# Two rotating mask tiles in place of three in a fused decoder layer, the freed space left empty

## The chip, the core and the metric

The kernel runs on one core of a Trainium2 chip. The metric is the device time of one execution in microseconds (us). The kernel before took 1540.39 us as the median of three runs (1539.06 to 1541.62). That is the figure that every change is measured against.

## What is computed

One decoder layer for 16 sequences of 100 tokens, width 128, against a context of 1444 rows per sequence. The reference, cut to its three residual steps:

```python
x = x + attn(layernorm(x), WQ, WK, WV)                  # banded self attention
x = x + xattn(layernorm(x), ctx, ctx, mask, W_Q, ...)   # 16 heads of 64, 1444 keys
x = x + ffn(layernorm(x), Wg, W1, ...)                  # 16 experts, top 2, and a shared one

def xattn(input_Q, input_K, input_V, attn_mask, ...):
    scores = einsum('bhqd,bhkd->bhqk', Q, K) / sqrt(64)
    scores = where(attn_mask[:, None, :, :], -10000.0, scores)
    return einsum('bhqk,bhkd->bhqd', softmax(scores), V) ... @ W_out.T + b_out
```

The mask is an input with one byte for each sequence, query and key: 16 x 100 x 1444.

## The kernel before

**Stages.** First the weights of the two attentions are folded together (`first_*`), then comes the cross attention of the 16 sequences, called batches here, one period of some 82 us each, and last the expert network. Self attention is worked off beside the cross attention, two sequences at a time, in what the code calls units: unit 0 in the first stage, unit 1 in the period of batch 0, units 2 to 7 each from an even batch into the odd one after it.

**Tiles.** The 1600 rows of a batch's score matrix (100 queries by 16 heads) are cut into 12 tiles of 128 rows, 8 queries by 16 heads, and one of 64 rows. So there are 13 tiles in a batch and 208 in all. For each tile, in this order:

- SP loads the tile's mask bytes, 128 x 1444 (180.5 KB), each query's row repeated for the 16 heads (`load_mask`, L900).
- POOL makes `bias = mask * -1e30 + c` from it (`make_bias`, L991). `bias` has two tiles of its own.
- PE makes the scores in two halves (L1257), DVE adds the bias and takes the row minimum of each half (L1142), ACT takes the exponential (L1073), POOL normalises (L1013, L1015), PE transposes the result (L1273), ACT and DVE split it into a high and a low part (L1082, L1157), and PE multiplies it by the context (L1297).

**The mask tiles rotate.** `MSLOTS` (L50) is their number, three. Tile n, counted through all batches, lies in slot n mod `MSLOTS`. Its load waits until the bias that read the slot's previous mask is made, which is the bias of tile n - `MSLOTS`; POOL's bias waits for the load by a semaphore of the slot.

**Order on the engines.** Each engine's order is fixed when the program is written: `ORDER` and the functions `act_order`, `dve_order` and `pool_order` lay it out by position in a period. DVE's list puts the statistics of unit 1 (`stat1`, L412) between the two halves of batch 0's first tile, and they wait for the unit's rows of x, `unit_x`. SP runs its list of loads and stores in order, and a load that waits holds back all that stands behind it. That list is `emit` under `@block.sync` (L910 to L946). The mask load of tile t stands first in step t, and the other transfers of the step behind it:

```python
def load_mask(b, t):                                              # L894
    n = b * NT + t
    wait(sp, bias_ready, n, 1, 1 - MSLOTS)                        # at least n + 1 - MSLOTS biases made
    sp.dma_start(masks[n % MSLOTS][0:rows_of(t), :], ...)
for t in range(NT):                                               # L916
    if here(b, 0):
        load_mask(b, t)
    if t == 2 and b == 0:
        load_context(1)                        # nat: 704 KB and three small pieces, L275, L278
        store_x1(sp, w, 0, x1_dram)            # unit 0's rows leave unit_x, L483
        load_x(sp, w, 1, x)                    # unit 1's rows enter it, once the store has landed, L490
        load_x1(0, 0)
    if t == 2 and 1 <= b <= CHUNKS // 2:
        clear(2 * b - 2)                       # waits for a POOL step behind the bias of tile 1
```

Behind later mask loads of a batch stand, in odd batches, the store of a unit's normalised rows (step 5, `store_n2`, L497) and the turn of its row constants through DRAM (step 6, `turn_c`, L504, L506, which PE reads at L367); in all, the load of the next batch's query rows (step 7, `load_rows`, L512, which PE reads at L1318) and a second `clear` (step 8). The next batch's context is loaded at the start of a period.

Of the kernel before, what the change touches and what calls it, by code (L numbers as in the profile page):

```python
# [46 lines left out]
NSTEP = len(STEPS)  # L47
PSLOTS = 6
TSLOTS = 3
MSLOTS = 3  # L50
QROUNDS = H // 2
PREP = 3 + QROUNDS
UNIT_AT = (11.5, 14.5, 16.5, 23.5, 36.2, 11.5, 14.5, 36.2)
# [6 lines left out]
def rows_of(t):  # L60
    return 128 if t < FT else HALF
# [723 lines left out]
def attention(nc, x, ctx_in, mask, wq_s, wk_s, wv_s, W_Q, b_Q, W_K, b_K, W_V, b_V, W_out, b_out,  # L785
# [4 lines left out]
    with ExitStack() as ctx:  # L790
        def sb(name, shape, dt=F32):
            return ctx.enter_context(nc.sbuf_tensor(name, shape, dt))

        def sem(name):
            return ctx.enter_context(nc.semaphore(name))

        def pair(name, shape, dt=F32):
            return [sb(f"{name}{i}", shape, dt) for i in range(2)]
# [6 lines left out]
        x1 = pair("x1", [S, D])  # L805
        masks = [sb(f"mask{i}", [128, SK], U8) for i in range(MSLOTS)]
        bias = pair("bias", [128, SKP])
# [14 lines left out]
        x1_in = [sem("x1_in0"), sem("x1_in1")]  # L822
        mask_in = [sem(f"mask_in{i}") for i in range(MSLOTS)]
        ctx_split = sem("ctx_split")
# [45 lines left out]
        def wait(engine, sem, b, per, plus):  # L870

            if b * per + plus > 0:
                engine.wait_ge(sem, b * per + plus)
# [7 lines left out]
        with nc.Block() as block:  # L881
            @block.sync
            def _(sp):
# [10 lines left out]
                def load_mask(b, t):  # L894
# [3 lines left out]

                    wait(sp, bias_ready, n, 1, 1 - MSLOTS)
                    sp.dma_start(masks[n % MSLOTS][0:rows_of(t), :],  # L900
                                 mask[b, q0:q0 + nq, :].unsqueeze(1).to_broadcast([nq, H, SK]))\
                        .then_inc(mask_in[n % MSLOTS], 16)

# [50 lines left out]
            def _(pool):  # L954
# [24 lines left out]
                def emit(b, odd):  # L979
                    def make_bias(db, t):  # L980
# [4 lines left out]
                        if t == 0:  # L985

                            pool.wait_ge(w.c_set, bb // 2 + 1)
                        pool.wait_ge(mask_in[m % MSLOTS], 16 * (m // MSLOTS + 1))

# [1044 lines left out]
```

## Time and profile before

| | us |
|---|---|
| median of three runs | 1540.39 |
| the profiled execution | 1540.29 |
| its span, from the first to the last instruction | 1538.1 |
| PE (matmuls) busy in it | 1439.2 |
| DVE busy | 1132.7 |
| POOL busy | 990.6 |
| ACT busy | 882.0 |

The profiled execution is one of the kernel's ordinary ones: it lies 0.1 us from the median. Some 2.2 us lie outside of its span. The page says for each engine how long it was busy, and in 40 slices of the span when. What an engine waited for is in the view of waits, and the order of single instructions in the timelines.

### The profile page before, as it was taken

What the parts mean: (1) busy time and instruction counts of PE and PEld (TensorE: products, weight loads), DVE (VectorE), ACT (ScalarE), POOL (GpSimd) and SP (SyncE); (2) the same over time, 40 slices, a digit from 0 to 9 for tenths busy, and PEclk for the clock granted to TensorE, in tenths of its full rate; (3) what the DMA queues carried; (4) which work ended last, traced back from release to release, by engine and by line L of the source; (5) the groups of instructions that cost most, each with busy time, mean ns of one, the idle gap of its engine ahead of it and who ended that gap; (6) DMA issues with size and microseconds to landing.
All of it is one profiled execution on the core that took longest, in us unless ns stands there. A gap on an engine that the chain in (4) does not pass through costs nothing. (4 is left out here: it accounts for less than half of the span.)

```text
span 1538.1 us, 30012 instructions
## 1 busy us (share of the span) xinstructions
PE 1439.2 (94%) x10546; PEld 1381.0 (90%) x10546; DVE 1132.7 (74%) x2768; ACT 882.0 (57%) x1663; POOL 990.6 (64%) x1127
## 2 busy tenths in 40 slices
PE   7799999999999999999999999999999999966696
PEld 6699999999999999999999999999999999955585
DVE  4687777777787877787877777777878686758565
ACT  2465666656565656565656656566656565616453
POOL 4675767666675757575757676766767675426564
PEclk8899999999999999999999999999999999967898
DMA  4211111111111111121111111111111101024322
GB/s 107 60 49 48 54 41 54 39 42 56 36 58 47 55 37 45 45 62 36 59 45 57 36 55 36 48 45 30 54 43 49 38 30 35 4 77 144 84 64 90
DMA packets 99981, 80.45 MB, mean 52 GB/s; under 512 B 16905, under 2 KB 98650, under 8 KB 99834
## 3 DMA queue, kind: packets, MB, share of 16 engines
q1 hardware_dynamic: 95098, 73.11, 16.1%
q0 software_dynamic: 2112, 4.29, 0.8%
q8 instruction: 85, 1.39, 0.4%
q10 hardware_dynamic: 2624, 1.14, 0.3%
q14 instruction: 62, 0.51, 0.1%
HBM read 67.37 MB, written 11.15 MB: 51 GB/s over the span
## 5 line engine op out<-in xcount | busy, mean ns | idle before, releaser
L1082 ACT CAST pT_hi<-banks 128x512 fp32r<-128x512 f32 (+1 forms) x672 | 362.4, 542 | 297.4 <-PE banks L1273 292.1
L1157 DVE TENSOR_TENSOR pT_lo<-banks,pT_hi 128x512 fp32r<-128x512 f32 (+1 forms) x576 | 360.2, 626 | 232.5 <-ACT pT_hi L1082 228.0
L1013 POOL TENSOR_SCALAR probs<-probs,row_inv 128x1408 f32<-128x1408 f32 x192 | 279.3, 1455 | 225.5 <-DVE row_inv L1149 225.3
L1273 PE MATMUL banks<-ident,probs 128*128 128x128 f32 (+1 forms) x2304 | 366.3, 274 | 18.9 <-DVE pT_lo L1157 9.6
L991 POOL TENSOR_SCALAR bias<-mask,c_all 128x1444 f32<-128x1444 uint8 (+1 forms) x208 | 307.0, 1476 | 118.3 <-DVE nmax L1142 107.5
L1073 ACT ACTIVATE probs<-probs,nmax 128x1448 f32<-128x1448 f32 x192 | 289.8, 1509 | 79.1 <-DVE nmax L1142 78.7
L1297 PE MATMUL banks<-pT_hi,ctx_hi 128*128 128x256 f32 (+1 forms) x1056 | 325.5, 308 | 0.3 <-DVE ctxT_lo L1183 0.3
L1273 PEld LDWEIGHTS banks<-ident,probs 128*128 128x128 f32 (+1 forms) x2304 | 266.9, 139 | 40.9 <-DVE pT_lo L1157 25.8
L1297 PE MATMUL banks<-pT_hi,ctx_lo 128*128 128x256 f32 (+1 forms) x1056 | 301.4, 285 | 0.0
L1297 PE MATMUL banks<-pT_lo,ctx_hi 128*128 128x256 f32 (+1 forms) x1056 | 300.3, 284 | 0.0
L1257 PE MATMUL banks<-ctxT_hi,qh 128*128 128x362 f32 x832 | 240.7, 370 | 6.2 <-POOL ql L1050 6.2
L1257 PE MATMUL banks<-ctxT_hi,ql 128*128 128x362 f32 x832 | 207.2, 330 | 0.0
L1257 PE MATMUL banks<-ctxT_lo,qh 128*128 128x362 f32 x832 | 206.6, 330 | 0.0
L1297 PEld LDWEIGHTS banks<-pT_hi,ctx_hi 128*128 128x128 f32 x1056 | 199.9, 189 | 0.7 <-issue 0.6
L1297 PEld LDWEIGHTS banks<-pT_lo,ctx_hi 128*128 128x128 f32 x1056 | 199.5, 189 | 0.0
L1297 PEld LDWEIGHTS banks<-pT_hi,ctx_lo 128*128 128x128 f32 x1056 | 198.4, 188 | 0.0
L1142 DVE CUSTOM_DVE_ANT_0 probs<-banks,bias,nmax 128x724 f32<-128x724 f32 x192 | 184.8, 962 | 5.1 <-PE banks L1257 4.3
L1142 DVE CUSTOM_DVE_ANT_0 probs<-banks,bias 128x724 f32<-128x724 f32 x192 | 172.7, 900 | 5.7 <-PE banks L1257 5.7
L1257 PEld LDWEIGHTS banks<-ctxT_lo,qh 128*128 128x128 f32 x832 | 149.1, 190 | 0.0
L1257 PEld LDWEIGHTS banks<-ctxT_hi,ql 128*128 128x128 f32 x832 | 148.6, 190 | 0.0
L1257 PEld LDWEIGHTS banks<-ctxT_hi,qh 128*128 128x128 f32 x832 | 126.8, 192 | 8.7 <-issue 6.3
L1103 ACT CAST qh<-qf 128x200 fp32r<-128x200 f32 x120 | 66.1, 551 | 92.0 <-DVE qf L1199 92.0
(290 smaller groups left out, 2307.8 us busy)
## 6 DMA issues: line engine op xcount, KB each, us to landing
mask<-in_mask_BxSxS_bk SPq DMA_DIRECT2D x192, 180.5 KB
nat<-in_ctx SPq DMA_DIRECT2D x16, 704.0 KB
up_raw<-in_L_ffn_W SPq DMA_DIRECT2D x32, 128.0 KB, 2.6
xs_dram<-empty SPq DMA_DIRECT2D x20, 130.0 KB, 1.7
rows<-xs_dram SPq DMA_DIRECT2D x10, 260.0 KB
down_raw<-in_L_ffn_W SPq DMA_DIRECT2D x16, 128.0 KB, 2.6
t_both<-yk_dram SPq DMA_DIRECT2D x3, 512.0 KB, 4.9
mask<-in_mask_BxSxS_bk SPq DMA_DIRECT2D x16, 90.2 KB
```

The costliest lines, as they stand in the source:

```text
L991: pool.tensor_scalar(bias[(t + i) % 2][0:n, 0:SK], masks[m % MSLOTS][0:n, :], MASKED, c_all[0:n, bb, t:t + 1], ALU.mult, ALU.add).then_inc ...
L1013: pool.tensor_scalar(prob(j)[0:n, 0:FIRST], prob(j)[0:n, 0:FIRST], rinv[0:n, s:s + 1], 1.0, ALU.mult, ALU.mult)
L1073: act.activation(prob(j)[0:n, 0:SKP], prob(j)[0:n, 0:SKP], ACT.Exp, bias=nmax[0:n, 1, s:s + 1], scale=-1.0, accum_out=rsum[0:n, s:s + 1]). ...
L1082: act.copy(pT_hi[tslot(i, j)][:, 0:width], banks[:, T_BANK + j % 2, 0:width]).then_inc(turned_hi, 1)
L1103: act.copy(dst, qf_of(b + db, n)).then_inc(prep_hi, 1)
L1142: dve.tensor_tensor_reduce(prob(t)[0:n, cs].rearrange("p (a k) -> p a k", a=2), src, bias[(t + i) % 2][0:n, cs].rearrange("p (a k) -> p a ...
L1157: dve.tensor_tensor(p_lo, turn, p_hi.bitcast(F32), ALU.subtract).then_inc(turned_lo, 1)
L1257: last = pe.matmul(banks[:, S_BANK + c, 0:CW], qpart[:, rows], kpart[:, c * CW:(c + 1) * CW], start=first, stop=qpart is ql[i])
L1273: last = pe.transpose(banks[0:m, T_BANK + j % 2, at_col:at_col + 128], prob(t)[:, c0:c0 + m], ident[:, :])
L1297: last = pe.matmul(banks[:, out_bank(g), 0:width], stationary[:, k, :], moving[tslot(i, j)][:, cs], start=(k == 0 and stationary is ctx_hi ...
```

## The change

One constant. Two mask tiles and two slot semaphores are made in place of three, the wait in `load_mask` asks for n - 1 biases in place of n - 2, and the slot of a tile is n mod 2. No other tile takes the freed bytes.

```diff
 PSLOTS = 6
 TSLOTS = 3
-MSLOTS = 3
+MSLOTS = 2
 QROUNDS = H // 2
```

## Rows read from the trace of the kernel before

**Rows 1.** The page, part 1: busy time, share of span, instructions by engine.

```profile
PE 1439.2 (94%) x10546; PEld 1381.0 (90%) x10546; DVE 1132.7 (74%) x2768; ACT 882.0 (57%) x1663; POOL 990.6 (64%) x1127
```

**Rows 2.** Waits: who <- for whom: us in total, times, longest; POOL's bias, SP's mask load.

```profile
POOL bias L991 <- DVE nmax L1142: 107.5, 109, 2.1
...
SPq L900 <- POOL bias L991: 714.9, 151, 8.3
```

**Rows 3.** Timeline of POOL, batch 6, tiles 9 to 11: start us, us, instruction.

```profile
586.77 1.48 POOL L991 TENSOR_SCALAR bias<-mask,c_all 128x1444 f32<-128x1444 uint8 x1
...
590.95 1.47 POOL L991 TENSOR_SCALAR bias<-mask,c_all 128x1444 f32<-128x1444 uint8 x1
...
596.75 1.48 POOL L991 TENSOR_SCALAR bias<-mask,c_all 128x1444 f32<-128x1444 uint8 x1 [1.06 <-DVE nmax L1142]
```

**Rows 4.** One mask load: SP's issue, and GB/s in 40 slices of 603.4 to 607.4.

```profile
603.45 0.59 SPq L900 DMA_DIRECT2D mask<-in_mask_BxSxS_bk  x1
...
GB/s 0 0 0 0 0 0 0 0 0 0 0 0 0 0 87 29 14 116 101 188 188 144 202 202 188 188 144 43 15 0 0 0 0 0 0 0 82 0 0 0
```

**Rows 5.** Timeline of SP's issues at the start of batch 0.

```profile
32.92 1.98 SPq L900 DMA_DIRECT2D mask<-in_mask_BxSxS_bk  x3
41.42 0.41 SPq L275 DMA_DIRECT2D nat<-in_ctx  x1
41.88 1.45 SPq L278 DMA_DIRECT2D nat<-in_ctx  x3
48.85 0.30 SPq L483 DMA_DIRECT2D x_dram<-unit_x  x1
51.11 0.30 SPq L490 DMA_DIRECT2D unit_x<-in_x  x1
```

**Rows 6.** Timeline of POOL there: the biases of tiles 0, 2 and 3.

```profile
49.51 1.47 POOL L991 TENSOR_SCALAR bias<-mask,c_all 128x1444 f32<-128x1444 uint8 x1
...
58.40 1.47 POOL L991 TENSOR_SCALAR bias<-mask,c_all 128x1444 f32<-128x1444 uint8 x1
...
61.95 1.47 POOL L991 TENSOR_SCALAR bias<-mask,c_all 128x1444 f32<-128x1444 uint8 x1
```

**Rows 7.** Timeline of DVE there: unit 1's statistics and the half of scores behind.

```profile
55.17 0.48 DVE L412 BATCH_NORM_STATS2 unit_stats<-unit_x 100x6 f32<-100x128 f32 x2
56.16 0.97 DVE L1142 CUSTOM_DVE_ANT_0 probs<-banks,bias,nmax 128x724 f32<-128x724 f32 x1 [0.51 <-PE banks L1257]
```

**Rows 8.** GB/s of all DMA in 40 slices of 40 to 60, 0.5 us each.

```profile
GB/s 0 0 0 0 2 228 81 173 346 349 303 70 0 0 0 0 0 0 0 96 114 11 0 0 108 194 71 159 156 49 139 147 58 0 0 0 0 0 0 0
```

**Rows 9.** DMA issues of the whole span: KB each, median us from issue to landing.

```profile
n2hi_dram<-unit_qT SPq DMA_DIRECT2D x8, 100.0 KB, 2.0
n2lo_dram<-unit_xnT SPq DMA_DIRECT2D x8, 100.0 KB, 2.5
...
c_dram<-probs SPq DMA_DIRECT2D x1, 4.0 KB, 5.8
```

**Rows 10.** Windows: us, busy time of the engines, granted TensorE clock, DMA share, GB/s.

```profile
57.00:60.00 3.00, 1.52 (x9) 1.22 (x8) 2.58 (x10) 1.60 (x2) 2.21 (x3) 1.00 0.00 0
60.00:64.00 4.00, 3.28 (x12) 2.83 (x13) 2.13 (x6) 1.81 (x3) 3.81 (x4) 0.57 0.15 46
64.00:68.00 4.00, 4.00 (x30) 3.87 (x29) 2.35 (x5) 1.97 (x3) 2.52 (x3) 1.00 0.14 46
```

**Rows 11.** Timelines: SP's loads of constants and query rows, and PE's first use.

```profile
633.15 0.32 SPq L506 DMA_DIRECT2D unit_pr<-c_dram  x1
...
653.10 0.24 PE L367 MATMUL banks<-ident,unit_pr 26*128 26x26 f32 x1
...
716.69 0.62 SPq L512 DMA_DIRECT2D n<-n2lo_dram  x1
...
743.52 0.34 PE L1318 MATMUL banks<-n,A_hi 128*128 128x200 f32 x1
```

**Rows 12.** One instruction on six tiles that lie apart: ns shortest/median/longest.

```profile
L1013 POOL TENSOR_SCALAR probs<-probs,row_inv x192: 1440/1452/1540, 60.0 to 1332.0; 128x1408 f32<-128x1408 f32 x192
```

## The prediction

> **What bounds the kernel now.** I read the page's busy times first. PE is busy for 1439.2 us of a span of 1538.1 [rows 1], far above DVE, POOL and ACT, so in the long middle of the span, where it has next to no gaps, another engine's delay costs only as far as PE runs out of work. The second view is that of waits, for the instruction that reads the mask tiles. POOL's bias waits for DVE to give back a bias tile, 107.5 us over 109 times, and no row has it waiting for a mask DMA; SP's mask load, on the other side, waits for POOL's bias, 714.9 us over 151 times, at most 8.3 us at once [rows 2]. So the mask ring is ahead: SP stands at a full ring. With one slot fewer it stands longer, and the question is not the mask alone, but whatever else SP is to issue and for whom. I therefore went through SP's list against the timelines: each load that stands behind a mask load, and the start of the instruction that uses it.
>
> **The mask tiles themselves, at nothing.** The load of tile n may now start when bias n-2 is made instead of n-3. The tightest tile of the steady batches is the eleventh. Bias 9 of batch 6 ends at 586.77 + 1.48 = 588.25 and bias 11 starts at 596.75 [rows 3]: 8.50 us for a transfer whose last bytes pass 2.9 us after 603.40, 2.85 us after its issue at 603.45 [rows 4]. 5.6 us are left, and the pattern repeats in the batches. In batch 0 the biases follow faster, and there it is the issue that counts; I come to it. What hides the transfer is one whole tile of POOL's and PE's work; if that cover were gone, each tile would pay up to 2.85 us.
>
> **What stands behind the mask loads in later batches, at nothing.** Each load moves later by one step of the bias, 4 to 6 us. The turned constants are loaded at 633.15 and first used at 653.10, the next batch's query rows at 716.69 and 743.52 [rows 11]: 20 us and 27 us ahead, so after a delay of 6 us and a landing of 2 to 2.5 us (100 KB transfers [rows 9]; these are smaller) more than 11 us are left. The context is loaded more than half a period ahead. The `clear` of step 2 waits for bias 1 and that of step 8 for bias 7; a mask load behind them now asks for no more than the same bias, so these two waits stay where they are.
>
> **The addresses, at nothing.** The tiles allocated behind the masks move down. POOL's normalisation runs on six tiles that lie apart at 1440 to 1540 ns, median 1452 [rows 12], so a place in the row is worth little. As bounds I take plus or minus 0.3 us: I count no effect.
>
> **The start of batch 0, where it costs.** Here there is no step of slack. Today mask loads 0, 1 and 2 are issued together at 32.92. Behind the third stand the context of batch 1 (41.42 and, in three pieces, to 41.88 + 1.45 = 43.33), the store of unit 0's rows (48.85) and, once that store has landed, the load of unit 1's rows into the same tile at 51.11 [rows 5]. DVE takes their statistics at 55.17, without an idle gap before them [rows 7]. A load of 100 KB lands, by the stores of that size, 2.0 to 2.5 us after its issue [rows 9]; I take 2.2, so 53.3, which is 1.9 us ahead of its use. This is the thin place.
>
> With two slots mask load 2 must wait for bias 0, which ends at 49.51 + 1.47 = 50.98 [rows 6]. Nothing behind it passes. Step by step:
>
> - Mask load 2 at 51.0, and 0.65 us for its issue (three took 1.98).
> - The context's four issues from 51.65 on, 43.33 - 41.42 = 1.9 us, so the store is issued at 53.6 in place of 48.85: 4.75 us later.
> - If the store moves as it does today, it is done 51.11 - 48.85 = 2.26 us later, at 55.85, and unit 1's rows land at 55.85 + 2.2 = 58.1. DVE, which came to them at 55.2, would stand 2.9 us.
> - But the context is in front of it. Its bytes run from 42.5 to past 45.5 in the slices [rows 8], so it is done about 4.4 us after its first issue: 51.65 + 4.4 = 56.05, and the mask's 180 KB just ahead can add up to 0.7. A store whose data waits for that is done some 1.3 us after, at 57.4 to 58.0; the rows land at 59.6 to 60.2 and DVE stands 4.4 to 5.0 us.
>
> Whether a transfer waits for those in front of it the trace shows in one place: a store of 4.0 KB, issued in the first stage behind the weights, took 5.8 us to land, where 100 KB alone take 2.0 to 2.5 [rows 9]. So I take the second case.
>
> The Trainium skill, "DMA: Bandwidth & Descriptors", section "Queues, rings and completion order", says that each DMA engine takes the descriptors of one queue in the order in which they were put there, and that only their ends can overtake each other. That row agrees; by this rule the stall is the 4.4 to 5.0 us, without it 2.9.
>
> Behind the waiting statistics stands, on DVE, the second half of tile 0's scores. Today it starts at 56.16 and has waited 0.51 us for PE [rows 7]; that much of the stall is covered. The rest is D = 3.9 to 4.5 us, 4.2 in the middle, and 2.4 without the queueing. Who waits for that: ACT's exponential of tile 0, PE's fourth half of scores, which needs the second one taken, POOL's step of the unit and then its bias 2 at 58.40. All the work that PE has there hangs on this chain, since there is no batch before to fill in: it is busy for only 1.52 us of 57 to 60 [rows 10]. So D is added PE idle time. Later idle time can't take it back, since all the engines' later work is moved by the same D, and PE's work has not become less.
>
> Next in line are masks 3 and 4. SP reaches mask 3 after the unit's loads, at about 58.4, so it lands by 61.3; bias 3 comes at 61.95 + D = 66 [rows 6]. That holds.
>
> **The sum.** 0 for the masks, 0 for the later loads, 0 for the addresses, 4.2 for the start. On the profiled execution's 1540.29, which is 0.1 us from the median, this gives 1544.5 us; for 3.4 to 4.9 us, 1543.7 to 1545.2. A measurement of this kernel tells about 0.2%, 3.1 us, from no change.
>
> **The rivals.** *Two are enough.* The mask needs 2.85 us and has 8.5, and a delay at the start might be made good in a span where much is off the critical path. For it speaks that no bias waits for a mask; against it, that the unit's rows have only 1.9 us to give and the store is moved by 4.75. It gives 1540.4, and it decides if the rows land by 55.2.
>
> The Trainium skill, "Trainium Kernel Development and Optimization", section "Best Practices", asks for double buffers, so that a transfer lies beside work. By that rule the third tile is spare and the time stays; the trace agrees as far as the mask's own transfer goes, and the rule is silent on what a queue holds behind the waiting load.
>
> *The store slips past the context.* Then D is 2.4, 1542.7 us, not told from no change. It decides if the store lands within 2.5 us of its issue. The 4 KB row speaks against it; for it, that the store moves the other way, from SBUF to DRAM, while the context is read.
>
> *PE's clock.* Today it is granted at 1.00 from 57 to 60, at 0.57 on average from 60 to 64 and at 1.00 after that [rows 10]; 0.5 is the 1.2 GHz level. The fall follows a stretch where PE was busy for half the time. A longer gap may move it. If the slow stretch falls into the new gap, the 3.28 us of matmuls from 60 to 64 take 3.28 x 0.57 = 1.9 us, 1.4 less: D = 2.8, 1543.1 us, within 0.2%. If a second slow stretch follows, over the dense 4.00 us of 64 to 68, it adds up to 4.0: 1548.5 us.
>
> *The ring is late everywhere.* If a mask took over 8.5 us to land, every tile would pay; for 1 us on 195 tiles that is 1735 us. No row comes near to it.
>
> **How the numbers follow.** The forecast, 1544.5 with 1543.7 to 1545.2, gets 0.48; the second slow stretch 0.10; the late ring 0.02. These are slower, 0.60. Two are enough gets 0.15, the store that slips past 0.15, the clock that gives back 0.06: within 0.2%, 0.36. For faster no mechanism is left that would outweigh the stall; 0.04 stands for what the moved transfers may do unseen. The range takes in the store that slips past and most of the second slow stretch, and leaves out most of no change: 1541.0 to 1548.0.
>
> **What the profile will show.** Right: SP's mask load 2 at 51.0, the store of unit 0's rows at 53.6 and the load of unit 1's at 57.4 to 58.0; DVE idle before L412 for 4.4 to 5.0 us, put down to the DMA of `unit_x`; from batch 1 on all biases, scores and steps moved by one and the same amount; no wait of POOL for a mask. Wrong: the store lands in 2.3 us; DVE's wait is there, but by batch 1 the shift is gone; waits of L991 for a mask, or of PE for query rows, in later batches; a granted clock after 64 that differs from the one before.

## The result: 0.41% slower, and where the time went

The changed kernel takes 1545.05 us (1544.53 to 1547.57), the kernel before 1540.39 (1538.03 to 1541.62). The ratio is 1.0041, with a 95% interval of 1.003 to 1.0052, so the loss is 6.3 us (4.6 to 8.0). The two medians, of seven executions each, are 4.7 us apart, at the lower end of that interval. The forecast was 1544.5 us. The profiled execution of the changed kernel took 1547.46 us, 2.4 over its median, with a span of 1545.7; that of before took 1540.29 with a span of 1538.1. The trace therefore has 7.6 us to explain, and it can be followed stage by stage.

Page of the changed kernel, busy time of the engines, against [rows 1]:

```profile
PE 1444.9 (93%) x10546; PEld 1388.1 (90%) x10546; DVE 1133.4 (73%) x2768; ACT 881.6 (57%) x1663; POOL 991.3 (64%) x1127
```

The same instructions run on every engine, and DVE, ACT and POOL are busy for as long as before, within 0.7 us. PE alone is busy for 5.7 us more. That is a first sign that not all of the loss is idle time.

View of waits of the changed kernel, against [rows 2]: who waits for whom, us in total, times, longest.

```profile
POOL bias L991 <- DVE nmax L1142: 109.1, 108, 2.8
...
SPq L900 <- POOL bias L991: 924.1, 186, 17.2
...
DVE unit_stats L412 <- DMA unit_x<-in_x: 4.8, 2, 4.4
```

SP stands 209 us longer at the full ring, and this costs nothing in itself: POOL still has no wait for a mask. What has grown is the last row, DVE's wait for unit rows: the kernel before has it once, with 0.6 us at the start of the kernel, and here there are 4.4 us more in batch 0 (the other 0.4 us is at the start).

SP's issues at the start of batch 0 in the changed kernel, against [rows 5]: start us, us, instruction.

```profile
51.36 0.59 SPq L900 DMA_DIRECT2D mask<-in_mask_BxSxS_bk  x1
52.05 0.41 SPq L275 DMA_DIRECT2D nat<-in_ctx  x1
52.52 2.85 SPq L278 DMA_DIRECT2D nat<-in_ctx  x3
55.41 0.33 SPq L483 DMA_DIRECT2D x_dram<-unit_x  x1
57.91 0.30 SPq L490 DMA_DIRECT2D unit_x<-in_x  x1
```

The mask's third load follows the end of bias 0 (51.33), and everything behind it comes later: the context by 10.6 us, the store of unit 0's rows by 6.56, the load of unit 1's by 6.80. The three small pieces of the context take 2.85 us in place of 1.45.

DVE there in the changed kernel, against [rows 7]; in brackets the idle time before and what ended it.

```profile
54.84 0.91 DVE L1142 CUSTOM_DVE_ANT_0 probs<-banks,bias 128x724 f32<-128x724 f32 x1 [5.67 <-PE banks L1257]
...
60.12 0.49 DVE L412 BATCH_NORM_STATS2 unit_stats<-unit_x 100x6 f32<-100x128 f32 x2 [4.36 <-DMA unit_x<-in_x]
60.64 0.97 DVE L1142 CUSTOM_DVE_ANT_0 probs<-banks,bias,nmax 128x724 f32<-128x724 f32 x1
```

The second half of the scores starts at 60.64 in place of 56.16: 4.48 us. The changed execution reached batch 0 later by 0.35 us (bias 0 at 49.86, [rows 6] 49.51), so the stall itself is worth **4.1 us**.

POOL's biases are good marks of the progress, since they wait for DVE and so for PE. In the changed kernel, the biases of tiles 2, 4 and 207 (the last one):

```profile
62.87 1.47 POOL L991 TENSOR_SCALAR bias<-mask,c_all 128x1444 f32<-128x1444 uint8 x1
...
72.52 1.48 POOL L991 TENSOR_SCALAR bias<-mask,c_all 128x1444 f32<-128x1444 uint8 x1 [2.77 <-DVE nmax L1142]
...
1331.99 1.48 POOL L991 TENSOR_SCALAR bias<-mask,c_all 64x1444 f32<-64x1444 uint8 x1 [1.62 <-DVE nmax L1142]
```

In the kernel before, the biases of tiles 4 and 207 (that of tile 2, at 58.40, stands in [rows 6]):

```profile
66.77 1.48 POOL L991 TENSOR_SCALAR bias<-mask,c_all 128x1444 f32<-128x1444 uint8 x1 [1.48 <-DVE nmax L1142]
...
1324.81 1.47 POOL L991 TENSOR_SCALAR bias<-mask,c_all 64x1444 f32<-64x1444 uint8 x1 [1.61 <-DVE nmax L1142]
```

The distance between the kernels is 4.47 us at tile 2, 5.75 at tile 4, and 7.18 at tile 207. So 1.28 us came in two tiles right behind the stall, and 1.43 us over the rest of the batches. With 0.35 at the start, 4.12 in the stall and 0.4 behind the batches that makes the 7.6 us. The 0.35 and the 0.4 are no part of the change's loss: over all 14 traces bias 0 comes between 47.68 and 51.33, and what lies behind bias 207 takes 208.2 to 214.3 us, 210.4 and 213.7 in two executions of the changed kernel itself. Single times scatter by that much. The distance from bias 0 to bias 207 agrees within 0.6 us in two executions of the kernel before and 0.2 in two of the changed one, and by it the change loses 6.8 us here (1282.13 for 1275.30). The 1.28 us have a view of their own.

Windows of the changed kernel, against [rows 10]: stretch, us, busy time of PE, weight loads, DVE, ACT, POOL, granted clock, DMA share, GB/s.

```profile
57.00:60.00 3.00, 1.18 (x5) 0.83 (x3) 0.00 (x0) 0.00 (x0) 0.00 (x0) 0.85 0.21 63
60.00:64.00 4.00, 2.18 (x6) 1.71 (x6) 3.38 (x11) 1.60 (x2) 1.84 (x2) 0.66 0.14 46
64.00:68.00 4.00, 2.89 (x9) 2.47 (x10) 2.33 (x6) 1.80 (x3) 3.71 (x5) 0.50 0.14 46
68.00:72.00 4.00, 4.00 (x19) 3.94 (x19) 0.95 (x3) 0.60 (x2) 1.75 (x2) 0.56 0.15 46
```

From 57 to 60 DVE, ACT and POOL do nothing at all: this is the stall. After it the clock lies at half (0.5 is the 1.2 GHz level) over all of 64 to 68 and most of 68 to 72, where PE is busy without a gap; before, it was back at 1.00 by 64.

### The profile page after: what moved, and what is told of

Same layout as the page of the kernel before. It is cut to its first block and busy times, and to the rows that moved or that the text cites. A ratio compares the mean times of both kernels' runs of the same rounds, so it can differ in the third digit from the quotient of the medians.

```text
span 1545.7 us, 30012 instructions
## 1 busy us (share of the span) xinstructions
PE 1444.9 (93%) x10546; PEld 1388.1 (90%) x10546; DVE 1133.4 (73%) x2768; ACT 881.6 (57%) x1663; POOL 991.3 (64%) x1127
```

## Experiments

Three causes are to be told apart: the stall of 4.1 us (is it the wait of mask load 2, and what does that hold up?), the slow growth of 1.4 us, and the clock.

### What stands behind the wait

**Block ahead of the wait.** Two tiles as in the change, but the block that stands behind mask load 2 is issued ahead of it.

```diff
-                        if t == 2 and b == 0:
+                        if t == 1 and b == 0:
```

> Two mask tiles as in the change, but the context of batch 1, the store of unit 0's rows and the load of unit 1's are put ahead of mask load 2 in SP's list, so that nothing of them waits for bias 0. Theory A (all of the loss is DVE's wait for unit 1's rows at the start of batch 0, and what PE's clock makes of it): 1540.4 us, 1539 to 1541.6, no wait of DVE for the load of unit_x, all biases from the third on where they are in the kernel before to 0.5 us. Theory B (the smaller ring itself, or the moved addresses, costs a little in every batch: the biases of the changed kernel fall behind from 5.7 us in batch 0 to 7.2 in batch 15): a shift that grows by 0.1 us a batch stays, 1541.5 to 1543 us. Theory C (two are enough and the measured 4.7 us has another cause): 1545.

Measured: 1541.08 us, ratio 1.0008 (0.9997 to 1.0019). DVE in this kernel:

```profile
54.84 0.48 DVE L412 BATCH_NORM_STATS2 unit_stats<-unit_x 100x6 f32<-100x128 f32 x2
55.83 0.97 DVE L1142 CUSTOM_DVE_ANT_0 probs<-banks,bias,nmax 128x724 f32<-128x724 f32 x1 [0.51 <-PE banks L1257]
```

The wait for `unit_x` is gone, and the 0.51 us for PE is as it was in [rows 7]. With two mask tiles the stall is not there when nothing urgent stands behind the third load. The time is the first theory's, but the biases are not where they were to 0.5 us: bias 4 comes 0.95 us later than in the kernel before and bias 207 2.28 us, so the growth of the second theory is there too. Both are followed below.

**One wait.** Three tiles, and only mask load 2 is told to wait for bias 0: the change's wait at the start, without its ring and without moved addresses.

```diff
-                    wait(sp, bias_ready, n, 1, 1 - MSLOTS)
+                    wait(sp, bias_ready, n, 1, 1 - (2 if n == 2 else MSLOTS))
```

> Three mask tiles as before; the one edit is that mask load 2 of batch 0 waits for bias 0, as it must with two. Theory A: the whole loss is back, 1545 us (1544 to 1547.6): DVE waits 4.2 to 4.6 us for unit_x at L412. Theory B: less than that, 1542 to 1544, and no growth of the shift over the batches. Theory C: 1540.4.

Measured: 1543.71 us, ratio 1.0028 (1.0017 to 1.0039), a loss of 4.3 us. DVE, and SP's issues:

```profile
58.72 0.49 DVE L412 BATCH_NORM_STATS2 unit_stats<-unit_x 100x6 f32<-100x128 f32 x2 [4.69 <-DMA unit_x<-in_x]
```

```profile
50.48 0.41 SPq L275 DMA_DIRECT2D nat<-in_ctx  x1
50.94 1.48 SPq L278 DMA_DIRECT2D nat<-in_ctx  x3
52.46 0.33 SPq L483 DMA_DIRECT2D x_dram<-unit_x  x1
56.46 0.30 SPq L490 DMA_DIRECT2D unit_x<-in_x  x1
```

This one wait makes the stall by itself, a little longer than the 4.2 to 4.6 us expected. The time lies in the range of the second theory (1542 to 1544), though its interval overlaps that of the change; by the marks from bias 0 to bias 207 this execution loses 4.8 of the change's 6.8 us. So the wait makes the greater part of the loss and not the whole of it. The small pieces were issued here in 1.48 us, and the store then took 4.0 us (52.46 to 56.46), where it takes 2.26 in the kernel before [rows 5].

**Unit first.** In the change's place, the store and the load of the unit's rows ahead of the context.

```diff
                             store_x1(sp, w, 0, x1_dram)
                             load_x(sp, w, 1, x)
+                            load_context(1)
```

> Two mask tiles; behind mask load 2 the store of unit 0's rows and the load of unit 1's come first and batch 1's context after them. Theory A: mask load 2 at 51.4, store at 52.0, landed at 54.3 (54.9 if it queues behind the mask's 180 KB), load landed at 56.5 to 57.1, and DVE, which is there at 55.8, waits 0.7 to 1.3 us; 0.5 of that is covered, so 1540.6 to 1541.2 us. So some 3.5 of the 4.4 us that DVE waits in the changed kernel belong to the context ahead of the store (its issues and its data), and the rest to mask load 2 alone.

Measured: 1544.59 us, ratio 1.0032 (1.002 to 1.0044), some 3.5 us more than expected. SP, then DVE:

```profile
51.98 0.48 SPq L483 DMA_DIRECT2D x_dram<-unit_x  x1
55.23 0.31 SPq L490 DMA_DIRECT2D unit_x<-in_x  x1
```

```profile
57.52 0.49 DVE L412 BATCH_NORM_STATS2 unit_stats<-unit_x 100x6 f32<-100x128 f32 x2 [1.93 <-DMA unit_x<-in_x]
```

The stall fell from 4.36 to 1.93 us, so the context had been in front. It didn't fall to 0.7 to 1.3, since behind the mask's 180 KB alone the store took 3.25 us. The rest of the miss is in the two terms that the expectation had not: from tile 2 to tile 4 this execution loses 1.1 us, and over the batches 1.4, as the change does.

**Store between.** The large piece of the context (704 KB by the page's list of DMA issues), then the store and the load, then the three small pieces: the store is issued early, but behind the large piece.

```diff
-                            load_context(1)
                             store_x1(sp, w, 0, x1_dram)
                             load_x(sp, w, 1, x)
+                            load_context(1, main=False)
```

(with `load_context(1, main=True)`, the large piece alone, ahead of the three.)

> Two mask tiles; behind mask load 2 the context's 704 KB piece alone, then the unit's store and load, then the context's three small pieces. It tells the data's queueing from the time of the issues: in the changed kernel the second small piece took 1.77 us to issue in place of 0.37. If a transfer waits for the data in front of it, as the prediction had it: store issued at 52.5, landed when the context's bytes are through, 57.0, load landed at 59.3, DVE waits 3.5 us, 1543.3 us. If it doesn't and the issues alone hold it up: store landed 2.3 to 2.5 us after its issue, at 55.0, load landed at 57.2, DVE waits 1.4 us, 1541.3 us.

Measured: 1544.75 us, ratio 1.0037 (1.0025 to 1.0049), a DVE wait of 4.42 us. SP:

```profile
52.31 0.41 SPq L276 DMA_DIRECT2D nat<-in_ctx  x1
52.78 0.63 SPq L484 DMA_DIRECT2D x_dram<-unit_x  x1
58.18 0.29 SPq L491 DMA_DIRECT2D unit_x<-in_x  x1
```

The wait and the time are above the 3.5 us and 1543.3 us of the queueing, and far from the 1.4 and 1541.3 of the other theory. The store, issued 2.6 us earlier than in the change, took 5.4 us and was no sooner done. Counted from the context's first issue, its end lies at 5.87 us here, at 5.86 in the change and at 5.98 with the one wait. So the data in front decides, not the moment of the store's own issue, and the three small issues cost the store nothing.

### The ring itself

**One tile.** One mask tile, the block ahead of the second load, two unused tiles in the place of the others.

```diff
-MSLOTS = 2
+MSLOTS = 1
...
+        pad_tiles = [sb(f"pad_tile{i}", [128, SK], U8) for i in range(2)]
...
-                        if t == 2 and b == 0:
+                        if t == 0 and b == 0:
```

> A single mask tile, the unit's transfers ahead of mask load 1, and unused tiles for the other two, so that the addresses are as before. Each mask load waits for the bias of the tile just before. By the timeline of the kernel before, the time from a bias to the next is under the 2.9 us of a transfer on 18 of 207 tiles, by 6.9 us in all, and DVE takes a bias 2.9 us or more after it is made. Theory A (the ring is no bound at all): the biases wait for mask DMAs some 7 us in total and the time stays within 0.1% of before, 1539.8 to 1541 us. Theory of the prediction's words, that a tile without cover pays up to 2.85 us: if POOL's delay is not hidden by DVE's slack, the 6.9 us come through, 1547 us.

Measured: 1539.13 us, ratio 0.9999 (0.9989 to 1.0008). The wait view of this kernel:

```profile
POOL bias L992 <- DMA mask<-in_mask_BxSxS_bk: 25.0, 24, 3.4
```

Now POOL does wait for masks, 24 times and 25 us in all, where the expectation had some 7 us, and the time doesn't show it. Not even the second tile is needed for the time. The forecast had put up to 2.85 us a tile on a lost cover. With one tile the next load starts only when a bias is done, yet most tiles leave it time enough; where it came late, the wait is 1.0 us on average and 3.4 at most, and its price in the whole time is not told from nothing.

### The addresses

**Block ahead, addresses kept.** The two-tile kernel with the block ahead, with an unused tile where the third mask had been, so that all tiles behind lie as before.

```diff
+        pad_tile = sb("pad_tile", [128, SK], U8)
```

> Two mask tiles, the unit's transfers ahead of mask load 2, and an unused tile of 1444 bytes behind the masks, so that all tiles behind lie where they lie in the kernel before. In the two-tile kernels so far the matmuls that read pT_hi and pT_lo are 1.0 to 1.7 ns longer each than with three tiles, and the biases fall behind by 0.1 us a batch. If the addresses make that: pT_lo x ctx_hi back at 279.4 ns (281.0 in the change), no growth of the shift over the batches, 1539.8 us as before, within 0.1%. If it is the ring of two: 281.0 ns and the growth of 1.4 us stay, 1541 us.

Measured: 1539.85 us, ratio 0.9998 (0.9988 to 1.0007): the time of the first theory.

**Three tiles, addresses moved.** The kernel before, with its third mask allocated behind `oT_lo`: the ring as before, and the tiles between the masks and that place (`bias`, `probs`, `pT_hi`, `pT_lo`, `oT_hi`, `oT_lo`) where the change has them. The small tiles behind `oT_lo` stay where they were, so the edit moves less than its expectation says.

```diff
+        masks = [sb(f"mask{i}", [128, SK], U8) for i in range(MSLOTS - 1)]
...
+        masks.append(sb("mask2", [128, SK], U8))
```

> Three mask tiles and every wait as before; the third is allocated behind all the others, so that the tiles behind the masks lie where the change puts them. No load waits longer than before. If the addresses cost: pT_lo x ctx_hi at 281.0 ns, the biases fall behind by some 0.1 us a batch to 1.4 us in all, 1541.2 us, 0.1% slower. If it is the ring of two: 279.4 ns, no growth, 1539.8 us.

Measured: 1539.79 us, ratio 0.9999 (0.9989 to 1.0008): the timing doesn't show the expected 1541.2.

**Half the distance.** As the first of these, with half of the unused tile ([128, 736]).

> As the two-tile kernel with the unit's transfers first, with an unused tile of 736 bytes behind the masks: the tiles behind lie 736 bytes below where they were before, between the two places tried. It asks whether the cost goes with the place. If only the 1472-byte place is bad, pT_lo x ctx_hi is at 279.4 ns and the time 1539.8; if every other place is worse than the old one, 281 ns and 1541.2; if this one is better, under 279 ns and below 1539.8 us.

Measured: 1538.81 us, ratio 0.9992 (0.9982 to 1.0002), not told from before. Of the three theories the first fits, by the 279.2 ns below.

What the times can't resolve, the traces do. The distance from the bias of tile 4 to that of tile 207 is free of the start:

| kernel | tiles behind the masks | tile 4, us | tile 207, us | between, us |
|---|---|---|---|---|
| before | as before | 66.77 | 1324.81 | 1258.04 |
| one wait | as before | 70.53 | 1328.38 | 1257.85 |
| block ahead, addresses kept | as before | 67.18 | 1325.02 | 1257.84 |
| half the distance | 736 bytes down | 66.78 | 1324.82 | 1258.04 |
| change | 1472 bytes down | 72.52 | 1331.99 | 1259.47 |
| block ahead | 1472 bytes down | 67.72 | 1327.09 | 1259.37 |
| unit first | 1472 bytes down | 69.77 | 1329.25 | 1259.48 |
| store between | 1472 bytes down | 72.84 | 1331.94 | 1259.10 |
| three tiles, moved | 1472 bytes down | 66.01 | 1325.32 | 1259.31 |

Two groups, 1257.84 to 1258.04 and 1259.10 to 1259.48, and what sets them is the place alone, with two tiles or three, with the stall or without. The traces of the next section fall into the same groups, each by its place: 1258.02 us with the tiles 736 bytes down, and 1259.30 with the matmuls in the stall, 1472 bytes down. (In the kernel with one mask tile the biases wait for masks and are no such marks.) Since the kernel with three tiles moved belongs to the second group, the tiles between the masks and `oT_lo` are enough for it. The matmuls that read the turned probabilities change with the place. Groups of instructions from 200 to 1100 us, one shape (line, engine, out<-in, count | busy us, mean ns | idle): before, change, three tiles moved, half the distance:

```profile
L1297 PE MATMUL banks<-pT_lo,ctx_hi 128*128 128x256 f32 x607 | 169.6, 279 | 0.0
```

```profile
L1297 PE MATMUL banks<-pT_lo,ctx_hi 128*128 128x256 f32 x607 | 170.6, 281 | 0.0
```

```profile
L1298 PE MATMUL banks<-pT_lo,ctx_hi 128*128 128x256 f32 x607 | 170.5, 281 | 0.0
```

```profile
L1298 PE MATMUL banks<-pT_lo,ctx_hi 128*128 128x256 f32 x607 | 169.5, 279 | 0.0
```

Busy time over count gives 279.4, 281.0, 280.9 and 279.2 ns. From 200 to 1324 us all 14 traces keep to this: 279.0 to 279.5 ns in the seven with the tiles as before or 736 bytes down, 281.0 to 281.3 in the seven with them 1472 bytes down. The growth per batch, 1.4 us over some 15 batches, is 0.1 us. Why this place is worse is not shown; only that it is the place. Nor is it shown how the longer matmuls become 1.4 us: the three groups of 256 columns (`pT_hi` twice, `pT_lo` once) are busy for some 3.3 us more from 200 to 1324, and PE's progress loses less than half of that. In the whole time the 1.4 us (0.09%) are no more than the half width of an interval. Three tiles moved comes out at 0.9999, at most 1.0008, just short of 1.4 us, so the times don't bear it out; only the marks in the traces do.

### The clock

**Matmuls in the stall.** The change, with 12 unread matmuls added where PE stands idle for the second half of tile 0, so that part of the idle time in front of the slow stretch is filled.

```diff
+                            if b + db == 0 and j == 3:
+                                for _ in range(12):
+                                    pe.matmul(banks[:, 4, 0:384], A_hi[:, 0, :],
+                                              A_hi[:, 0:3, :].rearrange("p a n -> p (a n)"), start=True, stop=True)
```

> The changed kernel with 12 matmuls of 384 columns more, whose result nobody reads, where PE stands idle while DVE waits for unit 1's rows. DVE's wait stays, 4.4 us. In the changed kernel three stretches of 3.4 us at half clock followed and moved bias 4 from 4.5 to 5.7 us behind. If PE's idle time in the stall brings them: the clock stays at 1.00 or falls for one stretch, bias 4 is 4.0 to 4.5 us behind the kernel before, 1543.5 us. If not: three stretches and 1545 us as in the change.

Measured: 1546.53 us, ratio 1.0053 (1.0036 to 1.0069). The added matmuls run from 57.56 to 59.81; 1.74 us of idle time are left before the next scores at 61.55, in place of the change's 3.49. The clock then stayed at 1.00 until 64.2, where in the change it fell at 61.3, so some 3 us of half clock are gone. But it was at half from there to 70.8 all the same, and tiles 2 and 4 are 9.65 us apart as in the change; bias 4 comes 6.10 us after bias 3 in both. So this stretch, at 64 to 71, is the one that costs, and the filling didn't take it away. Whether a stall filled to the end would, this run doesn't tell.

**Matmuls before batch 0.** The half-distance kernel with 28 unread matmuls added ahead of the first scores.

```diff
+                            if b + db == 0 and j == 0:
+                                for _ in range(28):
+                                    pe.matmul(banks[:, 2, 0:384], A_hi[:, 0, :],
+                                              A_hi[:, 0:3, :].rearrange("p a n -> p (a n)"), start=True, stop=True)
```

> The two-tile kernel with the unit's transfers first and the 736-byte pad, and 28 matmuls of 384 columns more, whose result nobody reads, ahead of batch 0's first scores, where PE stands idle for 6.2 us and the granted clock of the scores behind is 0.5. If the fall of the clock there comes from that gap, the first scores run at 1.00, each half in 1.0 us in place of 1.8 to 1.9, and no half-clock stretch follows in batch 0: 2 to 3 us less than the kernel without them, 1536 us. If the added matmuls themselves run at 0.5 and past the end of the gap, the first scores start up to 2 us later: 1541 us.

Measured: 1540.16 us, ratio 1.0012 (1.0001 to 1.0023): no gain, a miss. The first half of the expectation held: the clock was 1.00 from 38.4 to 62.3 us, the first scores ran at it, and biases 0 and 2 are 7.50 us apart in place of 8.88 in the half-distance kernel. But the half clock came all the same, at 62.3 to 69.1, over denser work, and biases 2 and 4 are 9.66 us apart in place of 7.99. What the first stretch gave, 1.38 us, the second took back with 1.67.

**Both kernels again, on one chip.** The two kernels unaltered, one behind the other.

> The kernel before, unaltered, looked at once more beside the change, for TensorE's clock alone. In its first profile the biases of tiles 2 and 4 are 8.37 us apart, with a half-clock stretch of 3.4 us; kernels without a stretch have 8.0, kernels with 6.8 us of it 9.65. If the length of the stretch goes with the kernel, the distance is 8.0 to 8.5 here. If it goes with the execution or the chip, it may come out at 9.6 here as well, or be 8.0 both here and in the change.

> The changed kernel, unaltered, on the same chip as the look at the kernel before. If the longer half-clock stretch belongs to the change, the biases of tiles 2 and 4 are 9.6 us apart again, 1.2 more than before. If it belongs to the execution or the chip, the two kernels agree within 0.3 us. In both cases DVE stands 4.3 to 4.7 us for unit 1's rows, and the distance from the bias of tile 4 to that of tile 207 is 1259.1 to 1259.5 us here and 1257.8 to 1258.1 in the kernel before, as addresses alone have set it so far.

One time each: 1535.57 us before, 1544.53 after (single executions; a third, of before, took 1541.63). Biases 2, 4 and 207 of before, then of the change:

```profile
56.56 1.47 POOL L991 TENSOR_SCALAR bias<-mask,c_all 128x1444 f32<-128x1444 uint8 x1
...
64.57 1.48 POOL L991 TENSOR_SCALAR bias<-mask,c_all 128x1444 f32<-128x1444 uint8 x1 [1.11 <-DVE nmax L1142]
...
1322.36 1.47 POOL L991 TENSOR_SCALAR bias<-mask,c_all 64x1444 f32<-64x1444 uint8 x1 [1.61 <-DVE nmax L1142]
```

```profile
63.27 1.47 POOL L991 TENSOR_SCALAR bias<-mask,c_all 128x1444 f32<-128x1444 uint8 x1
...
72.92 1.48 POOL L991 TENSOR_SCALAR bias<-mask,c_all 128x1444 f32<-128x1444 uint8 x1 [2.77 <-DVE nmax L1142]
...
1332.38 1.48 POOL L991 TENSOR_SCALAR bias<-mask,c_all 64x1444 f32<-64x1444 uint8 x1 [1.63 <-DVE nmax L1142]
```

Tiles 2 and 4 are 8.01 us apart before and 9.65 in the change; in the windows from 60 on the clock is 1.00 throughout before, and 0.70, 0.50, 0.52 from 60 to 72 in the change. DVE stands 4.50 us again, and tiles 4 and 207 are 1257.79 and 1259.46 us apart, in the same two groups as in the table. Taken over all kernels whose biases don't wait for masks, the distance from tile 2 to tile 4 is:

| | tiles 2 to 4, us |
|---|---|
| with the stall | change 9.65 and 9.65, one wait 9.06, unit first 9.50, store between 9.66, matmuls in the stall 9.65 |
| without it | before 8.37 and 8.01, addresses kept 8.00, moved 8.00, half 7.99; but block ahead 9.65, matmuls before batch 0 9.66 |

Every kernel with the stall has the long slow stretch; of those without it most have none or a short one, and two have it in full. The place of the tiles doesn't decide it: of the two, one has them 1472 bytes down and one 736, and each place has kernels with 8.0 us. So the stall goes together with 0.7 to 1.65 us of half clock, but it is not the only thing that brings it, and its cause stays open.

## Why the prediction was right, step by step

**The masks, at nothing: right.** No bias waits for a mask in the change, and with one tile in place of two the ratio is 0.9999. What was too high is the price of a lost cover, 2.85 us a tile: with one tile POOL loses that cover 24 times, 1.0 us a time, and the time shows none of it.

**The later loads, at nothing: right.** No wait of POOL, PE or DVE for constants, query rows or context has come up in the batches: from 76 to 1335 us no engine has a wait for a DMA, before or after. The step that these loads are moved by was put at 4 to 6 us; by the biases of the kernel before it is 4.15 to 8.90 us, and the 20 us of the tightest load cover that too.

**The start of batch 0: right, D = 4.1 us for 3.9 to 4.5.** Mask load 2 came at 51.36 for 51.0, the rows landed by 60.1 for 59.6 to 60.2, the store had landed by 57.91 for 57.4 to 58.0, the wait is 4.36 us for 4.4 to 5.0, at its lower end; all but the wait include the 0.35 us by which this execution came later. Less the 0.51 us that the prediction takes off, the wait alone gives 3.85; the rest up to 4.1 is DVE's, which reached the statistics 0.24 us later than that 0.35. Two numbers of the working have no row: the 1.3 us from the end of the context's data to the end of the store, and the step from D's 3.9 to 4.5 to the 3.4 to 4.9 us of the sum. The first held: from the context's first issue to the end of the store the prediction has 5.7 to 6.4 us in all, and the runs show 5.86, 5.87 and 5.98. One step is off in its form: the store was forecast to be issued at 53.6 and to take some 4 us, and it was issued at 55.41 and took 2.50, since SP's issue of the small pieces was itself held, 2.85 us for 1.45. The kernel with the one wait has the forecast's form (1.48 and 4.0), and the sum is the same, because the data in front decides in both.

**The addresses, at nothing: the step that failed.** The bound of 0.3 us was taken from POOL's normalisation on six tiles [rows 12], a row of another engine and of another use of the tile. PE's matmuls change with the place, by 1.0 to 1.7 ns each, and 1.4 us over the batches is what the traces show, five times the bound.

**The rivals.** *Two are enough* is right about the masks and wrong about the kernel: the kernel with the block ahead is what it describes, and the change is not. *The store slips past the context* is refuted by the store between: 5.4 us where it would have been 2.5. (The Trainium skill's rule on the order of a queue, in "DMA: Bandwidth & Descriptors", "Queues, rings and completion order", agrees with that 5.4 us.) *The clock* was put as all or nothing, a gain of 1.4 or a loss up to 4.0 us more; what came is a loss of 1.3 us in the profiled execution and 1.6 in the pair on one chip. Its second slow stretch did come, at 64 to 72, at a third of the price; whether the change brought it stays open. *The late ring* is refuted by the change itself, where no bias waits for a mask, and by the kernel with one tile, where the longest wait is 3.4 us.

**The signs.** Of the prediction's signs of being right, the stall, its releaser and the missing wait for masks came; that everything is moved by one and the same amount from batch 1 on did not, since the shift grows from 5.75 to 7.18 us. Of its signs of being wrong one came, the clock behind 64: 0.50 and 0.56 for 1.00.

The main term is right; that the forecast lies only 0.5 us from the median is luck in part. The two terms counted at nothing or left to a rival add 2.7 us in the trace, and the scatter of the single times, above all behind the last tile, is as large as they are: by the medians the loss is 4.7 us, by the marks 6.8. From bias 0 to bias 207, where the terms show without it, the traces add up: 1275.3 and 1274.7 us before, 1276.2 with three tiles moved, 1274.9 with the block ahead and the addresses kept, 1277.9 with the block ahead, 1280.1 with the one wait, 1282.1 and 1282.3 in the change. The ratio's 6.3 us (4.6 to 8.0) is above 4.2, and 4.1 + 1.4 = 5.5, with 0.7 to 1.65 of clock 6.2 to 7.2, lies within it. The one wait's 4.3 us and the block ahead's 1.2 us (ratio 1.0008) divide the loss in the same way, though the second of these is not told from none.

No version beats the kernel before: the best one with two tiles, half the distance, is at 0.9992 (0.9982 to 1.0002).

## What to carry to other kernels

A ring's depth is also the order of a queue: before a slot is taken away, go through everything that is issued behind the load that will now wait, above all where there is no slack (here the start), and move the urgent transfers ahead of the wait. The store that mattered here was to be timed from the end of the data in front of it, not from its own issue. And when tiles are taken out, put an unused tile in their place once: it tells what the change does from what the moved addresses do. When the effect is near the scatter of the times, measure between two marks in the trace that enclose it: here the whole times scatter by some us, and the marks of nine kernels fall into two groups 0.2 and 0.4 us wide.

## What was not expected of the hardware

- The place of a matmul's operand in SBUF: with the tiles between the masks and `oT_lo` 1472 bytes lower the 256-column matmuls on `pT_lo` took 281.0 ns in place of 279.4; at 736 bytes lower they took 279.2.
- SP's issue of a DMA can itself be held: three small pieces behind a mask and a 704 KB piece took 2.85 us in the change (2.94 in its second execution), but 1.48 behind the same two with the one wait; in the kernel before, 1.45. What holds it is not shown.
- A store of 100 KB that is issued right behind 180 and 704 KB took 5.4 us, behind 180 KB alone 3.25, and in the kernel before, where nothing was on its way, 2.26 (2.45 in its second execution).
- Unread matmuls in PE's idle time did not keep its clock up for long: with those in the stall it fell to half at 64.2 in place of 61.3, and with those before batch 0, which ended at 52.4, at 62.3. Tiles 2 and 4 were 9.65 us apart with the filled stall and without.
